# A hyperbolic edge pass over pairs of groups instead of single groups

## The reference

```python
x_src = x[src]
x_dst = x[dst]
msg = logmap(x_src, x_dst, c)
msg = msg * edge_weight[:, None]
agg = jax.ops.segment_sum(msg, dst, num_segments=N)
```

## Time and profile before

| | us |
|---|---|
| median of 3 runs | 7794.26 (7785.04 to 7800.03) |
| the profiled execution, its own time | 7782.6 |
| its span in the trace | 7780.9 |
[...]
| the edge pass in it, from its first gather to its last addition | 4337.9 to 5184.4 |

### The profile page before, as it was taken

One profiled execution on the slowest core, in us unless ns is written; L12 is line 12 of the kernel. 1 busy time (PEld: TensorE's weight loads), 2 busy tenths in 40 slices (PEclk: granted clock), 3 DMA queues, 4 the chain that ended last, 5 costly groups with the idle time before them and its releaser, 6 DMA issues. The chain is left out here.

```text
span 7780.9 us, 82688 instructions
## 1 busy us (share of the span) xinstructions
PE 4943.0 (64%) x21442; PEld 3404.9 (44%) x21443; DVE 3982.2 (51%) x11544; ACT 2332.1 (30%) x4547; POOL 3440.1 (44%) x3181
## 2 busy tenths in 40 slices
PE   1214966777772886667777467655996555455685
PEld 1103644555552554444554355544664323232474
DVE  8200025777777445677452577784435334343544
ACT  0002334554550112233212355543332222221122
POOL 4773015666662341777203455520003773676043
PEclk6555558988895897888885677777997767776687
DMA  2102432333332434555213222210002332333323
GB/s 46 28 21 69 137 110 80 97 96 95 94 92 65 129 114 62 161 161 164 76 39 86 75 69 71 68 35 14 17 8 70 93 92 60 93 92 92 103 79 103
DMA packets 377709, 633.66 MB, mean 81 GB/s; under 512 B 130352, under 2 KB 258451, under 8 KB 376033
## 3 DMA queue, kind: packets, MB, share of 16 engines
q0 software_dynamic: 146096, 360.51, 16.3%
q1 hardware_dynamic: 231005, 263.55, 12.9%
q10 hardware_dynamic: 308, 6.40, 0.3%
HBM read 474.19 MB, written 155.98 MB: 81 GB/s over the span
## 5 line engine op out<-in xcount | busy, mean ns | idle before, releaser
L784 POOL DMA_INDIRECT conv_rows<-rows_b,index x832 | 849.3, 1021 | 1228.6 <-SPq L2706 882.0
L816 DVE TENSOR_TENSOR acc<-acc,ps 125x257 f32 (+1 forms) x1664 | 701.1, 421 | 923.8 <-DMA acc<-slots,ffn_slot_of 379.8
L2752 PE MATMUL ps<-conv_rows,conv_weight_of 128*125 128x256 f32 x1664 | 624.9, 514 | 605.6 <-issue 269.7
L784 POOL DMA_INDIRECT gat_rows<-rows,index x416 | 558.6, 1343 | 818.8 <-POOLq L93 466.9
L2752 PEld LDWEIGHTS ps<-conv_rows,conv_weight_of 128*125 128x125 f32 x1664 | 359.7, 244 | 870.8 <-issue 538.3
L532 PE MATMUL ps<-front_L_gnn_W_t,front_attr_t 64*125 64x256 f32 x800 | 377.0, 648 | 419.3 <-issue 380.1
L784 POOL DMA_INDIRECT mpnn_rows<-rows_b,index x416 | 478.0, 1149 | 334.2 <-POOLq L1648 151.0
L333 POOL DMA_INDIRECT records_src<-by_src_edge_stage,by_src_edge_slot x400 | 410.1, 1025 | 449.2 <-DMA by_src_edge_stage<-edge_rows 177.9
L784 POOL DMA_INDIRECT hyp_rows<-rows,index x416 | 422.0, 1014 | 399.1 <-PE ps L2359 265.5
L2740 ACT ACTIVATE conv_weight_of<-conv_onehot_b,index 128x125 f32<-128x125 bf16 x832 | 251.5, 386 | 987.5 <-DVE conv_onehot_b L2724 754.4
L499 POOL DMA_INDIRECT records_dst<-front_back,front_dst_addr x400 | 417.4, 1044 | 214.4 <-issue 129.7
(11 more groups left out here) (591 smaller groups left out, 10529.6 us busy)
## 6 DMA issues: line engine op xcount, KB each, us to landing
mpnn_edge<-records_src SPq DMA_DIRECT2D x104, 512.0 KB
edge_rows<-front_edge_ring SPq DMA_DIRECT2D x100, 451.5 KB
by_src_edge_stage<-edge_rows SPq DMA_DIRECT2D x100, 451.5 KB
conv_rows<-rows_b,index POOLq DMA_INDIRECT x832
front_attr<-in_edge_attr SPq DMA_DIRECT2D x100, 112.0 KB
rows_b<-acc SPq DMA_DIRECT2D x15, 560.0 KB
second_w<-in_L_ffn_w SPq DMA_DIRECT2D x1, 8192.0 KB
slots<-mlp_y SPq DMA_DIRECT2D x56, 128.0 KB
```

Source lines behind the costliest of these rows:

```text
L784: pool.indirect_dma_start(out=rows[:, n % U, t, :], out_offset=None, in_=table, in_offset=bass.IndirectOffsetOnAxis(ap=ends[:, n * G + t:n ...
L816: dve.tensor_tensor(here, here, S.ps[0:P, t % banks, 0:width], ALU.add).then_inc(added, 1)
L2752: pe.matmul(S.ps[0:P, t, 0:D], weight_of[:, q.slot, t, :], rows[:, q.slot, t, :], start=True, stop=True).then_inc(summed, 1)
```

## The change

The pass works on 26 pairs of groups. The chain of `coefficients` runs once a pair, on columns of 16. The copies of weights and norms (`columns`), the two jobs on ScalarE and the signal that the coefficients are ready come once a pair as well. The slots for gathered rows and one-hots become six (`RING`), two of them in the room of `S.xT`; a gather of group n waits for the sums of group n - 6. The look-ups have four banks (`LB` = 4, banks 4 to 7), the sums three (`SB` = 3, banks 0 to 2), the transposes bank 3. All four engines' programs are written out.

VectorE's order is new: sixteen dots of the pair, with the additions of the first group of the pair before between the last eight; two compares for the next pair; then the chain, with the eight additions of the second group of the pair before in its gaps. The columns are made ahead of the dots, which waits for the gathers of both groups.

```diff
-                LB = 3
+            RING = 6
+            PAIRS = GROUPS // 2
+            PT = 2 * G
+            LB, SB, TURN = 4, 3, 3
+            FIRST = 4
...
+                def dots_done(k):
+                    return 2 * (k // PT + 1) + 2 * (k + 1)
...
-                    gather_groups(pool, ends, S.rows, rows, summed, gathered, go)
+                    for n in range(GROUPS):
+                        if n >= RING:
+                            pool.wait_ge(summed, (n - RING + 1) * G)
+                            pool.sem_inc(go, 1)
+                        for t in range(G):
+                            pool.indirect_dma_start(
+                                out=rows_of_pair(n // 2)[:, n % 2, t, :], out_offset=None, in_=S.rows,
...
+                    def columns(p):
+                        h = p % 2
+                        for n in (2 * p, 2 * p + 1):
+                            dve.wait_ge(gathered[n % RING], (n // RING + 1) * 16 * G)
...
+                    def dot(k):
+                        p, u, t = k // PT, k // G % 2, k % G
+                        h = p % 2
+                        dve.wait_ge(looked_up, k + 1)
+                        src = S.ps[:, FIRST + k % LB, 0:D + 1]
+                        dve.tensor_copy(X[:, h, u, t:t + 1], src[:, D:D + 1]).then_inc(dotted, 1)
+                        if k >= 2:
+                            dve.wait_ge(dotted, dots_done(k - 2))
+                        dve.tensor_tensor_reduce(junk[:, k % 2, :], src[:, 0:D], rows_of_pair(p)[:, u, t, 0:D],
+                                                 1.0, 0.0, ALU.mult, ALU.add, V[:, h, u, t:t + 1]).then_inc(dotted, 1)
+
+                    def add_up(k):
+                        n = k // G
+                        b = ids.of(Group(n, n % U, n // U, n), k % G)
+                        dve.wait_ge(summed, k + 1)
+                        if k:
+                            dve.wait_ge(added, k)
+                        here = S.acc[:, bass.ds(b, 1), 0:D + 1].rearrange("p a c -> p (a c)")
+                        dve.tensor_tensor(here, here, S.ps[0:P, k % SB, 0:D + 1], ALU.add).then_inc(added, 1)
+
+                    def coefs(p):
+                        h = p % 2
+                        gaps = iter([lambda k=k: add_up(k) for k in range((p - 1) * PT + G, p * PT)] if p else [])
...
-                        gaps = iter(add[:4] + dots[:LB] + add[4:] + dots[LB:])
...
+                    select(0)
+                    select(1)
+                    for p in range(PAIRS):
+                        columns(p)
+                        for k in range(p * PT, (p + 1) * PT):
+                            dot(k)
+                            if p and k % PT >= G:
+                                add_up(k - PT - G)
+                        if p + 1 < PAIRS:
+                            select(2 * p + 2)
+                            select(2 * p + 3)
+                        coefs(p)
+                    for k in range((PAIRS - 1) * PT, PAIRS * PT):
+                        add_up(k)
...
+                    for p in range(PAIRS):
+                        if p:
+                            scale(p - 1)
+                        if p + 1 < PAIRS:
+                            widen_one_hots(2 * p + 2)
+                        answer(p)
+                        if p + 1 < PAIRS:
+                            widen_one_hots(2 * p + 3)
+                    scale(PAIRS - 1)
...
+                    def look_up(k):
+                        n, t = k // G, k % G
+                        if t == 0:
+                            pe.wait_ge(turned_out, 2 * n + 2)
+                        b = ids.of(Group(n, n % U, n // U, n), t)
+                        if k >= LB:
+                            pe.wait_ge(dotted, dots_done(k - LB))
...
+                    def total(k):
+                        n, t = k // G, k % G
+                        pe.wait_ge(scaled, k + 1)
+                        if k >= SB:
+                            pe.wait_ge(added, k - SB + 1)
...
+                    for p in range(PAIRS):
+                        for k in range(p * PT, (p + 1) * PT):
+                            if p and k % PT >= G:
+                                total(k - PT - G)
+                            look_up(k)
+                        for k in range((p - 1) * PT + G, p * PT) if p else ():
+                            if k % G == SB and p + 1 < PAIRS:
+                                turn_one_hots(2 * p + 2)
+                            if k % G == G - 2 and p + 1 < PAIRS:
+                                turn_one_hots(2 * p + 3)
+                            total(k)
```

More of the change, by code:

```diff
@@ L2261, in coefs, with select @@
-                    def coefs(q):
-                        h = q.slot % 2
-                        add = [lambda t=t: accumulate(dve, S, q.previous(), ids, D + 1, 4, summed, added, [t])
-                               for t in range(G)] if q.since(1) else []
-                        more = not isinstance(q.n, int) or q.n + 1 < GROUPS
-                        dots = [lambda t=t: dot(q.next(), t) for t in range(G)] if more else []
-                        gaps = iter(add[:4] + dots[:LB] + add[4:] + dots[LB:])
+                    def select(n):
+                        dve.tensor_tensor(onehot_b[:, n % 2], bc_mid(S.iota[:, 0:P], G),
+                                          bc(local[:, n * G:(n + 1) * G], P), ALU.is_equal).then_inc(selected, 1)
@@ L2290, in ask @@
                             gap()
-                            dve.wait_ge(act_done, q.n * 4 + 2 * asked[0])
-                        dve.wait_ge(dotted, 2 * (q.n + 1) * (G + 1))
-                        if more:
-                            columns(q.next())
-                        coefficients(c, dve, lambda k: cols[:, h, k, :], rows[:, q.slot, :, D], X[:, h], Y[:, h],
+                            dve.wait_ge(act_done, p * 4 + 2 * asked[0])
+                        dve.wait_ge(dotted, dots_done((p + 1) * PT - 1))
+                        coefficients(c, dve, lambda k: cols[:, h, k], rows_of_pair(p)[:, :, :, D], X[:, h], Y[:, h],
                                      V[:, h], wts[:, h], ask)
@@ L2314, in _, with widen_one_hots @@
                 @block.scalar
                 def _(act):
-                    def answer(q):
-                        h = q.slot % 2
-                        for n, work in enumerate(jobs[2 * h:2 * h + 2]):
-                            act.wait_ge(act_ask, q.n * 2 + n + 1)
+                    def widen_one_hots(n):
+                        act.wait_ge(turned, n + 1)
+                        act.copy(onehot_t[:, n % 2],
+                                 S.ps[:, TURN, :].bitcast(BF16)[0:P, :].rearrange("p (t e) -> p t e", e=128))\
+                           .then_inc(turned_out, 1)
+                        act.copy(onehot_of(n), onehot_b[:, n % 2]).then_inc(turned_out, 1)
@@ new lines, in scale, with answer @@
+                    def scale(p):
+                        act.wait_ge(ready, p + 1)
+                        for u in range(2):
+                            for t in range(G):
+                                v = rows_of_pair(p)[:, u, t, 0:D]
+                                act.activation(v, v, ACT.Copy, scale=cols[:, p % 2, 3, u, t:t + 1]).then_inc(scaled, 1)
+                    def answer(p):
+                        for m, work in enumerate(jobs[2 * p:2 * p + 2]):
+                            act.wait_ge(act_ask, p * 2 + m + 1)
@@ L2353, in total @@
-                    def total(tiles):
-                        def stage(q):
-                            for t in tiles:
-                                pe.wait_ge(scaled, q.n * G + t + 1)
-                                if q.tile_since(t, 4):
-                                    pe.wait_ge(added, q.n * G + t - 3)
-                                pe.matmul(S.ps[0:P, t % 4, 0:D + 1], onehot[:, q.slot, t, :],
-                                          rows[:, q.slot, t, 0:D + 1], start=True, stop=True).then_inc(summed, 1)
-                        return stage
```

101 lines of the change are left out of this document (41 added, 60 removed).

## The result

The changed kernel takes 7769.2 us (median of 7 runs, 7765.3 to 7781.3) where the kernel before takes 7794.3 (7779.0 to 7800.0): ratio 0.9975, 95% interval 0.9964 to 0.9985. It is faster by 25 us, not by 182, and the prediction's range is missed. The profiled execution has a span of 7770.2 us, and its pass runs from 4336.4 to 5164.7 us, 18 us shorter than before.

A forecast was written before the change was run, and what follows sets the result against it. VectorE's program order was taken to bound the pass: 22.5 us of work plus 1.9 of wait, 24.4 a pair against 31.5, with start and end 182 us less: 7794.3 - 182 = 7612 us, range 7550 to 7690.

The forecast's parts named there:

- What bounds it: Pass over 52 groups: a ring of waits held together by VectorE's program order, 27.6 of 31.5 us per two groups.
- The durations: VectorE's work per pair: compares 2.25 us, sixteen dots 6.6, additions 0.42 each, chain 9.5; 22.5 in all without waits.
- Cost of the written-out programs: nothing: TensorE and ScalarE, looped before, become straight-line code in the pass; claimed to cost nothing, as with VectorE.
- What is left to 1.9 us of wait a pair: VectorE's wait among the dots, from TensorE starting at half clock: 12.6 us instead of 10.6, giving 24.4 a pair.
- The first pair needs about 20 us: Start of the pass: 11 us dots, 2.25 compares, 6.8 chain, so the second pair starts at 4381.25.
- Rival 3: Instruction-stream stalls in the pass while gathers run unpaused: 12 us a pair, some 7910 us; chance 0.08.
- More than 7.3 us a pair to be slower than before: Break-even for instruction-stream stalls in the pass: 182 us saved over 25 pairs, more than one such stall in each.
- Rival 1: TensorE's clock stays up in the pass: 22.5 us a pair, VectorE bound, 48 us less, 7564 us; chance 0.22.
- Rival 2: TensorE becomes the bound, at half clock for most of the dots: 26 to 30 us a pair, 7650 to 7750; chance 0.25.
- the 6.8 us at half clock: TensorE's clock at the head of each pair's dots, after a pause: 7.7 tiles at half clock, the other 12.3 at full.
- Wrong if the chain took 11 us or more: Sign against the forecast: VectorE's chain, expected at 9.4 to 9.6 us, lengthened by additions in it waiting for sums.
- Waits of 5 us with no releaser on VectorE: Sign against the forecast: VectorE waits that no semaphore explains, like the 5.51 us one at the old pass's start.

The follow-up runs named there:

- e4: The kernel before with TensorE's and ScalarE's programs written out, all else the same: 6922 us against 6923 for the kernel before on that chip.
- e14: The changed kernel with only the pass's first 48 gathers issued, all waits kept: 7606 us where the kernel before takes 7802; 22.8 us a pair.
- e5: The changed kernel unaltered, on a chip where the kernel before takes 6919 us: 6768 us, ratio 0.981, 23.1 us a pair.
- e6: The kernel before, unaltered, traced on a chip where updates do not come late: 6914 us, 14.8 us a group.
- e16: The changed kernel with a 192-column memset behind each gather, gathers 1.51 us apart: 6841 us, ratio 0.990 to the kernel before, 25.9 us a pair.
- e18: The changed kernel with gathers plain, each on its own tile's total, and paused, in one pass: 30.2, 27.7, 24.6 us a pair; 7702 us against 7797.

## Why the prediction was wrong

- **What bounds it** held: VectorE's program order, with waits in the ring. **The durations** held: additions 0.42, the last chain 9.3 us. On the prompt chip sixteen dots with eight additions took 10.6 us, the compares 2.2, the chain 9.9 instead of 9.5.
- **Cost of the written-out programs: nothing.** Held on a prompt chip (e4); on a late one nothing shows such a cost (e14).
- **"What is left to 1.9 us of wait a pair"** is the step that failed. It counted only the wait that a half clock makes, and no wait for an update. The profile has 8.2 us a pair, most of it behind late updates: where none come late, 1.9 are left (e5). That this is the forecast's number is chance, since TensorE's clock was full there and 1.0 of the 1.9 is "issue" ahead of additions. 24 pairs at 29.9 instead of 24.4 us (the copies of Y at 4413.64 and 5131.5) are 132 us of the 162 by which the pass missed (last addition over at 5164.7 instead of 5002.4); the end of the pass gave 2 back.
- **"The first pair needs about 20 us"** is the other 32, lost to late updates from 4364 on, beside 48 gathers without a pause: its successor's copy stands at 4413.64, not 4381.25. On the prompt chip it needed 21.1.
- **Rival 3** had the phenomenon: waits that no semaphore explains, while gathers run without pause. I read them as stalls of the instruction stream, and that was the error behind the two terms. With that cause, 750 us of undisturbed straight-line code spoke against it. With late updates as the cause, the same rows could have warned that such waits come wherever gathers are not paused, and that a tighter order will meet them in every pair. Its price of 12 us a pair was too high (5.5 over the forecast, 7.0 between the chips). "More than 7.3 us a pair to be slower than before" held: the pass missed by 162 us, 6.5 for each of 25 pairs, and that took nearly all of the gain.
- **Rival 1**, the clock that stays up, is what happened on the prompt chips: 1.00 during the dots of 22 of the 25 pairs, and 23.1 us a pair (it said 22.5). Rival 2's rise of the clock "within 7 us in each group" was not so in each: of 47 stretches at half clock that began between 4400 and 5130 us in the kernel before, 30 lasted 6.8 us and 17 lasted 10.2. On the late chip the mean during the dots was 0.84, and 1.00 in 24 of 26 pairs once the gathers were gone (e14): as I read it, TensorE, too, had sat waiting. So the 6.8 us at half clock that the forecast put at the head of each pair's dots are not there on either chip once no update is late.
- **What would show it.** "Wrong if the chain took 11 us or more": it took 11.5. "Waits of 5 us with no releaser on VectorE": 5.10, twice. GpSimd's wait for sums was to fall to about 1 us a group; on the prompt chip it fell to 1.3, on the late one it stayed at 4.7.

Open: what is saturated. In the kernel before, stages that issue indirect DMAs are longer on the late chip than in e6 (from their first instruction to their last the convolution 1352 us against 1233, the first stage 1105 against 670), the GRU, which issues none, is not (204 in both). Whether it belongs to those chips, to what else went on there, or to the taking of the records, which every run here had, no run could tell. The holes in the list of updates bear on it. With gathers running, about a quarter of the engines' increments and two thirds of the gathers' landings are missing on late chips; none are in e5, e6 or e16, nor in e14's stretch without gathers, and at 1.51 us between gathers (e18) it is 488 of 560 increments and 744 of 1696 landings that are on record. So where updates come late, their records are lost as well. That fits a path which carries both or a recording that gets in the way, and an execution without records would tell them apart. Nor was the kernel before tried on a late chip with its gathers taken away or slowed.

## What to carry to other kernels

Before an order is made tighter, look in the old trace for waits that no releaser explains, and ask what runs beside them. The order with slack hid the late signals here: its longest wait of a dot for its look-up was 0.6 us, the packed order's, by the same view, 3.7. No list of costs shows this cover. Price a hand-over between engines apart in stretches with back-to-back indirect gathers and without: on late chips a pair took 30.1 us with them and 22.8 without (e14). And let a burst of gathers that is not urgent, as the second and third pair's at the start, go out slower than it can: in e18 the first chain then began 38 us after the first gather instead of 67. If two chips disagree by 12% on the kernel before, measure a change on both.

## What the runs showed of the hardware

- On late chips semaphore updates of TensorE and VectorE arrived 2 to 4 us late while indirect gathers were issued 1.26 us apart (a pair 30.1 us); at 1.36 us a pair took 28.2, and at 1.51 us 24.6, with no wait for a look-up of over 1.2. In a run of 48 gathers the dots advanced in steps of 4.2 to 5.6 us, and an update of VectorE's own came 5.0 us late. The gathers' own data were on time: their last packet ended 2.46 us behind the issue on the late chip and 2.45 on the prompt one (medians of 416).
- On late chips the records of updates had holes while gathers ran (1408 of 1840 engine increments, 1831 of 5744 landings in 690 us of the changed kernel); on prompt chips none.
- The same program takes 12.6% longer on such a chip (7794 against 6919 us), and the same change is worth 0.25% there and 1.9% on the other.
- 53 MB of copies beside the gathers, as much again as the pass moves, added nothing to a pair of the changed kernel (30.1 us) and 1.9 us to two groups of the kernel before (31.3 to 33.2).
